# A 128-step recurrence: h's fold from three PSUM banks, its first triangles on ScalarE and GpSimd

## The chip, the cores and the metric

The program runs on one core of a Trainium2 chip. The metric is the time of one execution in device microseconds. "Before" is the median of three executions.

## What is computed

The reference is one block on x of shape (8, 128, 128): x plus causal latent attention over a recurrence of x, then plus six layers of window attention and gated feed-forward over a gated scan. Only the recurrence matters here:

```python
xw = einsum('ntd,dh->nth', x, Wx) + b
next_h = tanh(xw_t + prev_h @ Wh)      # 128 steps, 8 batches, D = 128
```

## The kernel before, in words

The kernel computes each step so that the sum over the 128 inputs is taken in a fixed order, one after another, with its roundings. For each output (a partition) and each of the 8 batches it needs the running sums of the products. It gets them in three parts: a **guess** (TensorE multiplies the weights by "triangles", copies of the step's vector masked so that column k holds the first k entries; one fp32 matmul gives all 128 prefix sums), a **rest** (the difference of neighbouring guesses is taken off the exact products, which TensorE makes from diagonal matrices of h or x, each split in an upper and a lower part), and the guess with its sign turned (**minus**). A reduction on VectorE, the **fold**, adds 3 x 128 numbers per batch, in the order rest, guess, minus. A program constant, OFFSET = 12, is added to guesses so that roundings fall where they should, and taken off again. Then VectorE evaluates tanh as a rational function with corrections.

There are two such sums per step: x's, which does not depend on h and is prepared a step ahead, and h's, which starts with x's result. Batches go in two halves of four. x's fold leaves its result where h's chain takes it in. PSUM has 8 banks of 512 columns: guesses of h in banks 0 and 1, rests of h in 2 and 3 (`REST_BANKS_H`), which x's guesses share (`SUM_BANKS_X`), x's rests in 4 and 6; small tiles of the tanh in 5 and 7. For the fold the three parts are laid side by side in SBUF (`adds`, in the space of the later layers' weights, stride 3).

Every engine has an order of its own, written by hand; semaphores join them. One step t:

- **VectorE**: `open_step` copies h to `h_now` (L1095), makes h's triangles of batches 0 and 1 (L1096), splits h in two parts (L1086, L1100). Then x's fold, first half (L1114), the difference of h's guesses, first half (L1108, L1109), x's fold, second half, four folds of h of two batches each (L1114, 128x768), tanh (L1130 to L1193). Its loop holds four steps; the others hold one.
- **ScalarE**: triangles of batches 2 and 3 (L783), h's guesses placed in `adds` (L798), `less_guess_of_h` (L803), lower diagonals of h, second half (L778), h's rests placed (`place_rests_h`, L821, 128x256 twice per half) with `place_minus_h` (L808) between; then for x of the next step, per half, the guess (L790) and its negative in the rest bank (L792), and last x's rests placed (L814).
- **TensorE**: h's guesses (`sums_h`, L1502), h's rests (`times`, L1487; the second half has first a matmul of the guess by the identity, L1551), x's guesses (`sums_x`, L1492, each after h's rest of that half has been placed), x's rests (L1512 and L1487), and `offset_h` (L1498), which opens the guess banks with the constant.
- **GpSimd**: h's triangles of the second half (L628), three diagonals of h (L642), h's copy to `hT` (L671), `minus_h` of the first half (L647), then for x, per half, triangles of step t + 2 (L628 again, after x's guess of that half), and per half the guess (L635) and its negative (L637) placed in `adds`.
- **SyncE** brings x's diagonals by DMA through a ring in HBM.

Behind the steps come latent attention and the layers, which the change does not touch, but for three reductions on VectorE at the end of the program (L1463 to L1467) whose result nobody uses.

## Time and profile before

| what | value |
|---|---|
| median of three runs | 3063.25 us (3061.85 to 3064.69) |
| the profiled execution's own time | 3067.32 us |
| its span | 3065.5 us |
| VectorE busy | 2690.4 us, 88% |
| PE (matmul) busy | 2581.4 us, 84% |
| GpSimd (POOL) busy | 2368.9 us, 77% |
| ScalarE (ACT) busy | 2261.6 us, 74% |
| mean granted TensorE clock | 0.986 |

The span runs from the first to the last instruction of the profiled execution. Busy times are of instructions in the engine; a matmul's row is longer than the time that it holds the queue, since the next one starts under it. The start of a row is in us from the span's start. "idle before <-releaser" is the time that the engine waited and whose result ended the wait.

### The profile page before, as it was taken

The page shows a single profiled execution, that of the slowest core. Times are in us where ns is not written, and L with a number is a line of the kernel's source. Part 1 is how long each engine was busy: PE and PEld are TensorE (multiplying, and loading weights), DVE is VectorE, ACT ScalarE, POOL GpSimd, SP SyncE. Part 2 cuts the span into 40 slices and gives each one's busy share as a digit, 9 for nine tenths or more (in the row PEclk, how much of TensorE's full clock was granted, in tenths as well). Part 3 has the DMA queues.
Part 4 walks back from the last instruction along what each step waited for, and adds up shares of the span by engine and source line. Part 5 has one row for each costly group of instructions (what it writes and reads, how often), then busy time and mean ns, then how long its engine had stood idle before and what let it go on. Part 6 is the DMA issues. An engine that isn't in the chain of part 4 may idle for free.

```text
span 3065.5 us, 51933 instructions
## 1 busy us (share of the span) xinstructions
PE 2581.4 (84%) x12402; PEld 1508.3 (49%) x12465; DVE 2690.4 (88%) x7345; ACT 2261.6 (74%) x4810; POOL 2368.9 (77%) x2545
## 2 busy tenths in 40 slices
PE   4878888887888888888878887876999999999997
PEld 2334433343433343333434333663666666667665
DVE  3999999999999999999999998656999999999996
ACT  3777777777777777777777776335888888888886
POOL 5777777777777777777777777007999999999994
PEclk9999999999999999999999999898999999999998
DMA  5333343333333333333333334200001010101000
GB/s 133 75 71 75 69 76 72 72 71 75 76 69 75 71 75 69 76 75 70 71 74 75 69 76 73 77 1 1 1 3 36 0 40 0 40 0 40 0 0 8
DMA packets 368014, 163.08 MB, mean 53 GB/s; under 512 B 285158, under 2 KB 298220, under 8 KB 367212
## 3 DMA queue, kind: packets, MB, share of 16 engines
q1 hardware_dynamic: 367980, 162.65, 25.7%
q8 instruction: 19, 0.31, 0.0%
q14 instruction: 15, 0.12, 0.0%
HBM read 156.81 MB, written 5.80 MB: 53 GB/s over the span
## 4 chain that ended last, share of the span: by engine, by line
DVE 33%; PE 22%; issue 20%; POOL 15%; ACT 6%; DMA 1%; POOLq 1%; SPq 1%; DVEq 0%; ACTq 0%
PE bank L1487 9%; POOL qk L714 8%; PE bank L1551 6%; DVE bank L1114 4%; PE bank L1502 4%; DVE bank L1109 3%; ACT qkv_w L798 3%; DVE sq L1089 3%; DVE bank L1089 3%; POOL rs L723 3%; DVE fix_trace L1180 3%; POOL qk L729 2%; ACT qkv_w L821 2%; DVE sq L1172 2%; DVE qkv_w L1114 1%
## 5 line engine op out<-in xcount | busy, mean ns | idle before, releaser
L628 POOL TENSOR_TENSOR kT<-upto,xT 128x512 f32<-128x512 f32 x260 | 270.1, 1039 | 380.8 <-PE bank L1492 380.8
L1114 DVE TENSOR_REDUCE bank<-qkv_w 128x2 f32<-128x768 f32 x512 | 466.1, 956 | 89.0 <-ACT qkv_w L821 74.1
L1487 PE MATMUL bank<-diag_h,w_part 128*128 128x512 f32 x1024 | 374.9, 488 | 161.5 <-DVE bank L1109 161.5
L1114 DVE TENSOR_REDUCE qkv_w<-qkv_w 128x4 f32<-128x1536 f32 x256 | 447.9, 1750 | 49.9 <-ACT qkv_w L814 32.7
L814 ACT COPY qkv_w<-bank 128x512 f32<-128x512 f32 x258 | 220.8, 856 | 255.3 <-PE bank L1487 255.3
L1487 PE MATMUL bank<-diag_x,w_part 128*128 128x512 f32 x1032 | 386.9, 496 | 13.4 <-DMA diag_x<-diag_ring 13.4
L642 POOL TENSOR_TENSOR diag_h<-eye,part 128x512 fp32r<-128x512 f32 x384 | 388.5, 1040 | 0.0
L1487 PEld LDWEIGHTS bank<-diag_h,w_part 128*128 128x128 f32 x1024 | 184.5, 190 | 410.4 <-issue 386.5
L1502 PE MATMUL bank<-qT,wh 128*128 128x256 f32 (+1 forms) x768 | 255.4, 468 | 149.8 <-DVE qT L1096 148.5
L723 POOL TENSOR_TENSOR rs<-rs,halfs 128x8 f32<-128x8 f32 x192 | 368.3, 1918 | 16.0
L1724 PE MATMUL bank<-qkv_w,xsT 128*128 (+1 forms) x576 | 308.6, 619 | 10.3 <-DVE rot_s L1336 8.0
L798 ACT ACTIVATE qkv_w<-bank,offset 128x512 f32<-128x512 f32 x256 | 230.8, 951 | 106.0 <-PE bank L1502 106.0
L1492 PE MATMUL bank<-kT,wx 128*128 128x512 f32 x516 | 276.6, 618 | 19.9 <-ACT qkv_w L821 19.9
L1512 PE MATMUL bank<-b,eye 128*128 128x512 f32 x516 | 273.9, 612 | 19.2 <-ACT bank L792 0.6
L635 POOL TENSOR_TENSOR qkv_w<-b,offset 128x512 f32<-128x512 f32 x258 | 269.2, 1043 | 14.6 <-ACT b L790 4.3
L1487 PEld LDWEIGHTS bank<-diag_x,w_part 128*128 128x128 f32 x1032 | 195.3, 189 | 161.7 <-issue 123.1
L821 ACT COPY qkv_w<-bank 128x256 f32<-128x256 f32 x512 | 214.5, 499 | 72.7 <-PE bank L1487 71.9
L714 POOL TENSOR_TENSOR qk<-rot_c,rot_s 128x512 f32<-128x512 f32 x192 | 244.2, 1272 | 25.9 <-DVE rot_s L1336 25.9
L1502 PEld LDWEIGHTS bank<-qT,wh 128*128 128x128 f32 x768 | 126.9, 188 | 235.4 <-DVE qT L1096 210.8
L637 POOL TENSOR_SCALAR qkv_w<-b 128x508 f32<-128x508 f32 x258 | 227.7, 882 | 17.5
L729 POOL TENSOR_TENSOR qk<-qk,rs 128x512 f32<-128x512 f32 x192 | 201.1, 1048 | 15.0
L790 ACT ACTIVATE b<-bank,offset 128x512 f32<-128x512 f32 x258 | 177.6, 688 | 25.5 <-PE bank L1492 19.0
(238 smaller groups left out, 6550.5 us busy)
## 6 DMA issues: line engine op xcount, KB each, us to landing
diag_x<-diag_ring SPq DMA_DIRECT2D x259, 512.0 KB, 7.2
qkv_w<-in_L_ffn_Wqkv SPq DMA_DIRECT2D x6, 1536.0 KB
diag_ring<-X SPq DMA_DIRECT2D x264, 4.0 KB, 5.6
diag_ring<-o_fin SPq DMA_DIRECT2D x8, 512.0 KB, 7.8
o_w<-in_L_ffn_Wo SPq DMA_DIRECT2D x6, 512.0 KB
w<-in_L_ffn_W SPq DMA_DIRECT2D x6, 341.0 KB
b<-in_L_ffn_b SPq DMA_DIRECT2D x6, 341.0 KB
w<-in_L_ffn_W SPq DMA_DIRECT2D x6, 128.0 KB
```

The lines of the kernel that those rows point to most:

```text
L628: pool.tensor_tensor(tri[n][:, rows, :], upto[:].unsqueeze(1).to_broadcast([P, 4, D]), src[:, rows].unsqueeze(2).to_broadcast([P, 4, D]), ...
L642: pool.tensor_tensor(diag[n][:, d, rows, :], eye[:].unsqueeze(1).to_broadcast([P, 4, D]), values.unsqueeze(2).to_broadcast([P, 4, D]), ALU ...
L714: pool.tensor_tensor(o, c_, s_[:, :, ::-1, :], ALU.add).then_inc(rot_sum, 1)
L723: link(pool.tensor_tensor(rs[:, c, :], rs[:, c, :], halfs[:, 0:8], ALU.pow), rs_ready, eight + (2 * c + 2))
L798: act.activation(adds[0][:, 4 * half:4 * half + 4, :, 1], bank[:, half, :].rearrange("p (n k) -> p n k", k=D), ACT.Identity, bias=offset[: ...
L821: act.copy(adds[0][:, rows, :, 0], bank[:, REST_BANKS_H[half], 2 * m * D:2 * m * D + 2 * D].rearrange("p (n i) -> p n i", i=D)).then_inc(r ...
L1114: return dve.tensor_reduce((pre, bias_at[0])[n][:, a:b], chain[n][:, a:b, :], AX_X, ALU.add)
L1487: return pe.matmul(dst, w_part[:, n, w], diag[n][:, d, a:b, :].rearrange("p n k -> p (n k)"), start=False, stop=True, skip_group_check=True)
L1492: pe.matmul(bank[:, SUM_BANKS_X[half], :], wx[:], tri[1][:, 4 * half:4 * half + 4, :].rearrange("p n k -> p (n k)"), start=True, stop=True ...
L1502: return pe.matmul(bank[:, half, (a - 4 * half) * D:(b - 4 * half) * D], wh[:], tri[0][:, a:b, :].rearrange("p n k -> p (n k)"), start=Fal ...
L1512: pe.matmul(rows, eye[:], guess_x[:, a:b, 0:D], start=False, stop=True, skip_group_check=True)
L1724: pe.matmul(bank[:, c % 2, :], xsT[:, par, :], w[:, at:at + BANK], start=True, stop=True).then_inc(qkv_ready, 1)
```

## The change

h's three parts stay in PSUM. Banks 0 and 3 hold its rests, 1 and 4 its guesses, 2 and 5 the negatives, and the fold of a half reads three neighbouring banks as one 128x4<-128x1536 reduction (`fold_h`). `place_rests_h`, GpSimd's `minus_h` and the four folds of two batches go; ScalarE writes both negatives to the PSUM banks (`place_minus_h`) and a contiguous copy of the guesses to SBUF (`copy_guess_h`). x's fold writes into the last column of the negatives' bank. The constant is taken off the guess by a one-row matmul (`less_offset_h`). x's rest banks are now 2 and 5, the small tiles' 6 and 7. `sums_x` waits for h's fold of the same half (`h_folded`). h's triangles of batches 0 and 1 are made by ScalarE in place of 2 and 3, those of 2 and 3 by GpSimd, ahead of its second half. VectorE's copy to `h_now` waits for `h_ready`. The three reductions at the end go. Renamed semaphores and x's index changes are left out below.

```diff
-REST_BANKS_H, REST_BANKS_X = (2, 3), (4, 6)
+REST_BANKS_H, GUESS_BANKS_H, MINUS_BANKS_H = (0, 3), (1, 4), (2, 5)
 SUM_BANKS_X = REST_BANKS_H
-OWN_BANKS = (5, 7)
+REST_BANKS_X = MINUS_BANKS_H
+OWN_BANKS = (6, 7)
...
-        adds = [qkv_w[:, n, :].rearrange("p (n i c) -> p n i c", n=NB, c=3) for n in range(2)]
-        bias_at = [tile[:, :, D - 1, 2] for tile in adds]
-        chain = [qkv_w[:, n, :].rearrange("p (n i) -> p n i", n=NB) for n in range(2)]
+        adds = qkv_w[:, 1, :].rearrange("p (n i c) -> p n i c", n=NB, c=3)
+        bias_at = adds[:, :, D - 1, 2]
+        chain = qkv_w[:, 1, :].rearrange("p (n i) -> p n i", n=NB)
+        guess_h = qkv_w[:, 0, 0:NB * D].rearrange("p (n k) -> p n k", n=NB)
...
+        minus_h = [bank_rows(which) for which in MINUS_BANKS_H]
+        links_h = [bank[:, first:first + 3, :].rearrange("p c (n k) -> p n k c", k=D) for first in REST_BANKS_H]
...
                 pool.wait_ge(h_static, this)
+                pool.tensor_tensor(tri[0][:, 2:4, :], upto[:].unsqueeze(1).to_broadcast([P, 2, D]),
+                                   h_now[:, 2:4].unsqueeze(2).to_broadcast([P, 2, D]), ALU.mult).then_inc(tri_h_mid, 1)
...
                 diagonal(0, 1, 0, part[:, 1, 0:4], diag_lower_h[0])
                 diagonal(0, 0, 1, part[:, 0, 4:8], diag_upper_h)
                 pool.tensor_copy(hT[:, :, bass.ds(value(pool, t + HT_AT), 1)].rearrange("p n a -> p (n a)"), h_now[:]).then_inc(h_ready, 1)
-                minus_h(counts[0])
                 later = at_step(value(pool, t + 2))
...
 
             def triangle_mid():
-                for n in (2, 3):
+                for n in (0, 1):
                     ins = act.activation(tri[0][:, n, :], upto[:], ACT.Copy, scale=h_now[:, n:n + 1])
-                ins.then_inc(tri_h_mid, 1)
+                ins.then_inc(tri_h_first, 1)
 
...
 
                 act.wait_ge(sum_ready[0], count)
-                act.activation(adds[0][:, 4 * half:4 * half + 4, :, 1], bank[:, half, :].rearrange("p (n k) -> p n k", k=D),
-                               ACT.Identity, bias=offset[:, 0:1], scale=1.0).then_inc(guess_placed, 1)
+                act.copy(guess_h[:, 4 * half:4 * half + 4, :], bank_rows(GUESS_BANKS_H[half])).then_inc(guess_copied, 1)
 
             def less_guess_of_h():
...
+                act.activation(bank[:, REST_BANKS_H[1], :], bank[:, GUESS_BANKS_H[1], :], ACT.Copy,
                                scale=-1.0).then_inc(less_guess_h, 1)
 
-            def place_minus_h():
-
-                act.activation(adds[0][:, 4:8, 0:D - 1, 2],
-                               bank[:, 1, :].rearrange("p (n k) -> p n k", k=D)[:, :, 0:D - 1], ACT.Identity,
-                               bias=offset[:, 1:2], scale=-1.0).then_inc(minus_placed[1], 1)
+            def place_minus_h(half):
+
+                act.activation(minus_h[half][:, :, 0:D - 1], bank_rows(GUESS_BANKS_H[half])[:, :, 0:D - 1], ACT.Copy,
+                               scale=-1.0).then_inc(minus_placed[half], 1)
 
...
+                copy_guess_h(0, counts[0])
+                act.wait_ge(split_h, this)
+                lower_h(4)
+                copy_guess_h(1, counts[1])
+                act.wait_ge(rest_placed_x, counts[1])
                 less_guess_of_h()
-                act.wait_ge(split_h, this)
-                lower_h()
-                place_rests_h(0, counts[0])
-                place_minus_h()
-                place_rests_h(1, counts[1])
-                act.wait_ge(sum_placed[1], counts[1])
-                act.wait_ge(rest_placed[1], counts[1])
+                act.wait_ge(diff_ready, this)
+                act.wait_ge(x_folded, this)
+                place_minus_h(0)
+                lower_h(6)
+                act.wait_ge(x_scanned, this)
+                place_minus_h(1)
+                act.wait_ge(sum_placed_x, counts[1])
+                act.wait_ge(rest_placed_x, counts[1])
                 take_sums_x(0, counts[2])
                 take_sums_x(1, counts[3])
...
+                    dve.wait_ge(h_ready, value(dve, this - 1))
                 dve.tensor_copy(h_now[:], h_own).then_inc(h_static, 1)
-                dve.tensor_tensor(tri[0][:, 0:2, :], upto[:].unsqueeze(1).to_broadcast([P, 2, D]),
-                                  h_own[:, 0:2].unsqueeze(2).to_broadcast([P, 2, D]), ALU.mult).then_inc(tri_h_first, 1)
                 n_u = upper(part[:, 0, :], h_own)
...
-                dst = bank[:, REST_BANKS_H[half], :].rearrange("p (n k) -> p n k", k=D)
-                placed = adds[0][:, 4 * half:4 * half + 4, :, 1]
-                dve.wait_ge(guess_placed, count)
-                dve.tensor_scalar(dst[:, :, 0:1], sums_[:, :, 0:1], -1.0, OFFSET, ALU.mult, ALU.add)
-                dve.scalar_tensor_tensor(out=dst[:, :, 1:], in0=sums_[:, :, 0:D - 1], scalar=-OFFSET, in1=placed[:, :, 1:],
-                                         op0=ALU.add, op1=ALU.subtract).then_inc(diff_ready, 1)
-
-            def fold(n, a, b):
-
-                return dve.tensor_reduce((pre, bias_at[0])[n][:, a:b], chain[n][:, a:b, :], AX_X, ALU.add)
+                rows = slice(4 * half, 4 * half + 4)
+                dst = bank_rows(REST_BANKS_H[half])
+                dve.wait_ge(guess_copied, count)
+                dve.tensor_scalar(dst[:, :, 0:1], guess_h[:, rows, 0:1], -1.0, None, ALU.mult)
+                dve.tensor_tensor(dst[:, :, 1:], bank_rows(GUESS_BANKS_H[half])[:, :, 0:D - 1], guess_h[:, rows, 1:],
+                                  ALU.subtract).then_inc(diff_ready, 1)
+
+            def fold_x(half):
+
+                rows = slice(4 * half, 4 * half + 4)
+                return dve.tensor_reduce(minus_h[half][:, :, D - 1], chain[:, rows, :], AX_X, ALU.add)
+
+            def fold_h(half):
+
+                return dve.tensor_reduce(pre[:, 4 * half:4 * half + 4], links_h[half], mybir.AxisListType.XY, ALU.add)
 
             def placed_x(halves):
-                dve.wait_ge(rest_placed[1], halves)
-                dve.wait_ge(sum_placed[1], halves)
+                dve.wait_ge(rest_placed_x, halves)
+                dve.wait_ge(sum_placed_x, halves)
 
             def products(dst, a, b):
...
-                    def placed_h(m):
-                        dve.wait_ge(rest_placed[0], quarters[m])
...
-                    fold(1, 4, 8).then_inc(x_scanned, 1)
-                    after(n_x)
-                    for m in range(4):
-                        placed_h(m)
-                        if m == 2:
-                            dve.wait_ge(x_scanned, this)
-                        n_h = step(fold(0, 2 * m, 2 * m + 2))
-                    after(n_h)
+                    fold_x(1).then_inc(x_scanned, 1)
+                    for half, done in ((0, x_folded), (1, x_scanned)):
+                        dve.wait_ge(done, this)
+                        dve.wait_ge(rest_ready[0], counts[half])
+                        dve.wait_ge(minus_placed[half], this)
+                        fold_h(half).then_inc(h_folded, 1)
+                    dve.wait_ge(h_folded, counts[1])
                     tanh()
                     open_step(value(dve, t + 2))
...
-            dve.tensor_reduce(small[:, 0:2], bank[0:SN, 0:3, 0:2 * D].rearrange("p c (n k) -> p n k c", k=D),
-                              mybir.AxisListType.XY, ALU.add)
-            dve.tensor_reduce(small[:, 2:4], bank[0:SN, 0:6:2, 0:2 * D].rearrange("p c (n k) -> p n k c", k=D),
-                              mybir.AxisListType.XY, ALU.add)
-            dve.tensor_reduce(small[:, 4:6], prob[0:SN, 0:6 * D].rearrange("p (c n k) -> p n k c", c=3, k=D),
-                              mybir.AxisListType.XY, ALU.add)
...
+            def less_offset_h(half):
+
+                return pe.matmul(bank[:, GUESS_BANKS_H[half], :], offset16[:, D:2 * D], offset16[:, 2 * D:], start=False,
+                                 stop=True, skip_group_check=True)
+
             def sums_h(half, a, b):
-                return pe.matmul(bank[:, half, (a - 4 * half) * D:(b - 4 * half) * D], wh[:],
+                return pe.matmul(bank[:, GUESS_BANKS_H[half], (a - 4 * half) * D:(b - 4 * half) * D], wh[:],
                                  tri[0][:, a:b, :].rearrange("p n k -> p (n k)"), start=False, stop=True,
                                  skip_group_check=True)
...
-                quarters = [value(pe, 4 * t + n) for n in (2, 4)]
                 pe.wait_ge(tri_h_first, this)
...
                 pe.wait_ge(tri_h_mid, this)
-                sums_h(0, 2, 4).then_inc(sum_ready[0], 1)
+                sums_h(0, 2, 4)
+                less_offset_h(0).then_inc(sum_ready[0], 1)
                 pe.wait_ge(tri_h_second, this)
-                sums_h(1, 4, 8).then_inc(sum_ready[0], 1)
+                sums_h(1, 4, 8)
+                less_offset_h(1).then_inc(sum_ready[0], 1)
 
                 for half in range(2):
...
                     else:
-                        pe.wait_ge(guess_placed, counts[1])
+                        pe.wait_ge(guess_copied, counts[1])
                         pe.wait_ge(less_guess_h, this)
-                        pe.matmul(bank[:, REST_BANKS_H[1], :].rearrange("p (n k) -> p n k", k=D)[:, :, 1:], eye[:],
-                                  adds[0][:, 4:8, 0:D - 1, 1], start=False, stop=True, skip_group_check=True)
-                    for d, made, count in ((0, diag_upper_h, counts[half]), (1, diag_lower_h[half], this)):
+                        pe.matmul(bank_rows(REST_BANKS_H[1])[:, :, 1:], eye[:], guess_h[:, 4:8, 0:D - 1], start=False,
+                                  stop=True, skip_group_check=True)
+                    for d, made, count in ((0, diag_upper_h, counts[half]), (1, diag_lower_h[half], (this, counts[1])[half])):
                         pe.wait_ge(made, count)
                         for w in range(2):
                             ins = times(bank[:, REST_BANKS_H[half], :], 0, w, d, 4 * half, 4 * half + 4)
                     ins.then_inc(rest_ready[0], 1)
                 for half in range(2):
-                    pe.wait_ge(rest_placed[0], quarters[half])
+                    pe.wait_ge(h_folded, counts[half])
                     sums_x(half, counts[2 + half])
                 for half in range(2):
                     rests_x(half, counts[2 + half], landed)
-                pe.wait_ge(minus_placed[1], this)
                 offset_h()
 
```

## Rows read from the trace of the kernel before

**Rows 1.** Busy time by engine (and instructions) in the steps' stretch, 39 to 1893.7 us.

```profile
39.00:1893.70 1854.70, 1495.21 (x4307) 732.56 (x4306) 1696.44 (x5694) 1360.82 (x2535) 1420.30 (x1520) 1.00 0.38 73
```

**Rows 2.** Line L1095: the whole run, then 500 to 1900 us.

```profile
L1095 DVE COPY h_now<-bank x129: 152/166/168, 13.0 to 1911.1; 128x8 f32<-128x8 f32 x129
...
L1095 DVE COPY h_now<-bank x97: 165/166/167, 501.7 to 1896.7; 128x8 f32<-128x8 f32 x97
```

**Rows 3.** Timeline of VectorE, one step: start us, us, what [idle before <-releaser].

```profile
1010.34 0.17 DVE L1095 COPY h_now<-bank 128x8 f32<-128x8 f32 x1
1010.42 0.41 DVE L1096 TENSOR_TENSOR qT<-upto,bank 128x256 f32<-128x256 f32 x1
...
1011.12 1.75 DVE L1114 TENSOR_REDUCE qkv_w<-qkv_w 128x4 f32<-128x1536 f32 x1
1013.05 0.17 DVE L1108 TENSOR_SCALAR bank<-bank 128x4 f32<-128x4 f32 x1 [0.17 <-ACT qkv_w L798]
...
1013.88 1.73 DVE L1114 TENSOR_REDUCE qkv_w<-qkv_w 128x4 f32<-128x1536 f32 x1
...
1018.14 1.82 DVE L1114 TENSOR_REDUCE bank<-qkv_w 128x2 f32<-128x768 f32 x2 [0.30 <-ACT qkv_w L821]
1020.00 0.17 DVE L1130 TENSOR_SCALAR bank<-bank 128x8 f32<-128x8 f32 x1
...
1024.84 0.17 DVE L1095 COPY h_now<-bank 128x8 f32<-128x8 f32 x1
```

**Rows 4.** Timeline of GpSimd (POOL), the same step.

```profile
1014.57 0.20 POOL L671 COPY hT<-h_now 128x8 f32 x1
1014.72 1.21 POOL L647 TENSOR_TENSOR qkv_w<-qkv_w,signs 128x508 f32<-128x508 f32 x1
...
1019.89 1.04 POOL L628 TENSOR_TENSOR kT<-upto,xT 128x512 f32<-128x512 f32 x1 [0.22 <-PE bank L1492]
...
1022.00 0.89 POOL L637 TENSOR_SCALAR qkv_w<-b 128x508 f32<-128x508 f32 x1
1022.97 1.04 POOL L635 TENSOR_TENSOR qkv_w<-b,offset 128x512 f32<-128x512 f32 x1
1024.08 0.87 POOL L637 TENSOR_SCALAR qkv_w<-b 128x508 f32<-128x508 f32 x1
```

**Rows 5.** Timeline of ScalarE (ACT), the same step.

```profile
1010.54 0.69 ACT L783 ACTIVATE qT<-upto,h_now 128x128 f32<-128x128 f32 x2 [0.48 <-DVE h_now L1095]
...
1013.71 0.65 ACT L803 ACTIVATE bank<-bank,offset 128x512 f32<-128x512 f32 x1
...
1017.61 0.85 ACT L821 COPY qkv_w<-bank 128x256 f32<-128x256 f32 x2 [0.56 <-PE bank L1487]
1018.47 0.69 ACT L790 ACTIVATE b<-bank,offset 128x512 f32<-128x512 f32 x1
...
1023.71 0.85 ACT L814 COPY qkv_w<-bank 128x512 f32<-128x512 f32 x1 [0.88 <-PE bank L1487]
```

**Rows 6.** Timeline of TensorE's matmuls (PE); first one matmul of L1492 alone.

```profile
1017.41 0.59 PE L1492 MATMUL bank<-kT,wx 128*128 128x512 f32 x1
...
1015.14 1.50 PE L1551 MATMUL bank<-qkv_w,eye 128*128 128x508 f32 x2
...
1018.59 1.12 PE L1492 MATMUL bank<-kT,wx 128*128 128x512 f32 x2 [0.15 <-ACT qkv_w L821]
...
1021.72 1.02 PE L1512 MATMUL bank<-b,eye 128*128 128x512 f32 x2
1022.17 1.50 PE L1487 MATMUL bank<-diag_x,w_part 128*128 128x512 f32 x4
1023.61 0.60 PE L1498 MATMUL bank<-offset 1*128 1x512 bf16 x2
```

**Rows 7.** Timeline at the program's end: reductions from PSUM, then from SBUF.

```profile
3059.10 0.94 DVE L1465 TENSOR_REDUCE small<-bank 64x2 f32<-64x768 f32 x1
3059.97 1.01 DVE L1467 TENSOR_REDUCE small<-prob 64x2 f32<-64x768 f32 x1
```

## What the change is expected to do

> **What bounds the kernel now.** I read the busy times of the recurrence's stretch first, then the period of its steps, then the timeline of one step engine by engine. In the stretch of the 128 recurrence steps VectorE is busy for 1696 of 1855 us, GpSimd for 1420, ScalarE for 1361 [rows 1]: VectorE leads, but nobody is free by much. The copy that opens a step (L1095) comes every (1896.7 - 501.7) / 96 = 14.53 us [rows 2]. The first two steps take what is left of 1898.1 us, 1898.1 - 126 x 14.53 = 67 us, and do something else (the ring is being filled); so 126 steps count.
>
> One step, from the copy at 1010.34 to that at 1024.84, is a nearly closed queue on VectorE [rows 3]: opening 0.78 (with 0.33 for the triangles of L1096), x's fold 1.75, difference 0.83 (from 1013.05 to 1013.88), x's other fold 1.73, four folds of h in two pairs of 1.82, then the tanh from 1020.00 to 1024.84, 4.84. Its waits are some 0.17 before the difference and such a 0.30 before each fold pair (the second pair is shown). A reader who stops here would say: VectorE bounds, take work from it.
>
> The other queue to read is GpSimd's [rows 4]. It handles x for step t+1 while VectorE does h of step t. Its triangle of x's second half waits for PE's sums (1018.59 + 1.12 = 1019.71 [rows 6]), and then four placements run to 1024.08 + 0.87 = 1024.95. The next step's h triangles are queued behind them, and the copy that releases these is at 1024.84. GpSimd is thus 0.1 us from being late.
>
> **The change, part by part.**
> VectorE loses the 0.33 of L1096 (two triangles); 2 x 1.82 + the 0.30 wait between the pairs become two folds of 128x4<-128x1536 from three banks. Their price: the same form at half length is there, 0.94 from PSUM and 1.01 from SBUF [rows 7]. A fold of 1536 takes 1.75 where one of 768 takes 0.955 (half of 1.82, plus the 0.045 of overlap), so 768 more elements cost 0.80, and I take 0.94 + 0.80 = 1.74 each, started 1.65 apart. Lower bound 1.65 (the SBUF fold less more than the PSUM gain of 0.07), upper 1.88 (twice 0.94). The Trainium skill (Perfetto Trace Analysis, Optimizing Scalar/DVE Operations) has an access overhead for VectorE of about 60 ns on SBUF and 125 on PSUM. By it, as an estimate, the two folds would cost 0.13 more per step, 16 us in all, and the time would be 3124; the two rows say the opposite for this very pattern, and I go by them.
> ScalarE loses the four strided placements of L821 that stood between PE and VectorE and the strided L798; its copies and negatives are now contiguous, 0.69 as L790 or 0.65 as L803 [rows 5]. Bounds 0.6 and 0.8 for the copies.
> PE reads the guess contiguously: two passes of L1551, with a stride of three, take 1.50, two of L1512 take 1.02 [rows 6], so some 0.46 is gained in its queue, where such a pass holds it for 0.43 (the 1.02 for two less the 0.59 of one, as at L1492). It adds two one-row matmuls (L1498: 0.60 for two, by estimate 0.23 in the queue and 0.37 to the end).
> GpSimd loses L647 (1.21), which stood in front of a wait anyway, worth nothing. It gains a triangle of 128x256 ahead of the one of 512: between 0.20 for 8 elements (L671) and 1.04 for 512 [rows 4], by length 0.61, in the queue 0.57; bounds 0.45 and 0.7. VectorE's new wait for h_ready is for a copy done 8 us earlier; only its own 0.05 or so counts, on an engine that will wait later in the step.
> **Moved:** PE's sums of x, half 1, waited for L821 (done 1017.61 + 0.85 = 1018.46) since it shares a bank with h's rest; now it waits for the second fold of h itself, the last thing before the tanh. Before, they were complete at 1019.71, 0.29 ahead of the tanh. Now they start 0.13 after the fold (as 1018.46 to 1018.59) and end 1.12 later, 1.25 after it. Behind them, in order, GpSimd's triangle and four placements, then the next step's h triangles, the later ones of which are on h's path. So x's loop closes through GpSimd:
>
> From the end of h's second fold,
> 1. to the end of x's sums: 0.13 + 1.12 = 1.25.
> 2. to GpSimd's next free start: 1024.95 - 1019.71 = 5.24, plus 0.08 (as from 1022.00 + 0.89 to 1022.97) = 5.32.
> 3. h's triangles, 0.57 + 1.04 = 1.61.
> 4. PE's second half: start 0.13 and first load 0.10 (as at L1492), two passes 0.86, one-row matmul 0.37 = 1.46.
> 5. ScalarE: start 0.04, guess copy 0.59 in the queue (0.69 less 0.10 of overlap), less_guess_of_h 0.57 (0.65 less 0.08), negative 0.65, 0.03 to VectorE = 1.88.
> 6. h's two folds, 1.65 + 1.74 = 3.39.
> Sum 14.91; I take 14.90. VectorE's own work in that period is 0.45 + 1.66 + 0.83 + 1.66 + 3.39 + 4.84 = 12.8, so it will wait about 2 us per step, nearly all of it before the difference. That wait also hides the 0.25 that VectorE's loop end costs in every fourth step (the mean of 14.53 against the 14.49 between the two copies of rows 3 has it), so 14.90 stands as the mean.
> Beside the steps: the three reductions at the end go (2.6 us, started 0.87 apart [rows 7]), and x's late last step adds about 1. Net -1.6.
> Change: (14.90 - 14.53) x 126 - 1.6 = 46.6 - 1.6 = +45. On the profiled execution, 3067.3 (span 3065.5 and 1.8 around it), that is 3112.3; the median of the runs stands 4.1 lower, so 3063.25 + 45 = 3108.
>
> **Rivals.**
> A, faster. GpSimd doesn't hold the loop (its spans are rough; its placements of x might really end earlier). Then x's loop closes through ScalarE: from h's last fold 0.13, PE's queue from L1492 to the last L1487 (1018.59 to 1023.67 is 5.08, less some 0.3 of waiting for ScalarE inside it: 4.8), then L814 0.04 + 0.75, the first triangles 0.69 (L783), PE 0.06 + 0.96 + 0.37 (its restart, four passes of 256 columns, the one-row matmul), copy 0.04 + 0.69, difference 0.11 + 0.66, x's fold 1.66, h's folds 3.39: 14.35 by rounding. That is -0.18 x 126 - 1.6 = -24, so 3039. It decides once GpSimd is 0.5 us faster. For it: VectorE's 2 us of slack. Against: the 0.1 us between GpSimd's last placement and the next step. 0.12.
> B, slower still. The eye matmul on the guess keeps the price of L1551, 0.66 a pass, since its output skips columns. Then h's second rest comes last: from the end of less_guess_of_h 0.05 + (0.86 + 0.46) + 1.10 (L1487's 1.50 less the 0.40 that its first lies under the pass before it) + 0.09 = 2.56 to the second fold, where the forecast has 0.58 + 0.03 + 1.65 = 2.26. So 0.30 more: 15.20, 0.67 x 126 - 1.6 = +83, 3146. 0.12.
> C, the folds at 1.88 instead of 1.74: 0.28 more, 15.18, 0.65 x 126 - 1.6 = +80, 3143. 0.08. Folds of 1.55 would be needed for no change; with the lower bounds of folds, triangle and copies together (-0.18, -0.12, -0.09) the period is 14.51 and the time 3063 - 4 = 3059. That all-low end, 0.06, is my "no change".
> The change does do what it says: L1096 and L821 are off VectorE's path in it; only the removed wait comes back elsewhere.
>
> **How the numbers follow.** Forecast 0.62, A 0.12, B 0.12, C 0.08, all-low 0.06. Most likely 3108. A measurement of this kernel tells 0.2%, 6 us, from no change. Faster by more: A, with 0.01 of the all-low end, 0.13. Same: 0.05. Slower: 0.82. The range leaves out A and the lower half of the all-low end below (0.15) and what lies above the centres of B and C (some 0.05): from 3062, which takes in the forecast with one or two lower bounds (folds at 1.65 and the triangle at 0.45: 14.60, 3070), to 3150.
>
> **What would show it.** In the profile after, per step: the copy to h_now every 14.9 us; VectorE idle 1.5 to 2 us before the difference, released by ScalarE's guess copy; GpSimd's first h triangle starting some 1.4 us after h_now's copy, not 0.25, with no idle time before it; PE's sums of x half 1 waiting for VectorE's fold for about 0.9 us; folds of 1.74; the busy time of VectorE down. Wrong, if GpSimd idles before h's triangles (A), if the rest of h's second half releases the last fold (B), if folds differ from 1.74 (C).

## The result and the profile after

The changed kernel takes 3273.4 us (median of 4 runs, 3271.4 to 3279.3) against 3063.4: 1.0687 times as long, 95% interval 1.0674 to 1.0700. That is 210 us more, where 45 were forecast. All ratios leave out executions in the chip's slower state or over 1.5% above the fastest of their kernel (two of the ten with the triangles back, 3121 and 3417 us, and one of the thirteen of the kernel before beside them, 4359). The head of its page, with the granted clock of TensorE in 40 slices:

```profile
span 3269.2 us, 51129 instructions
...
PE 2856.2 (87%) x12721; PEld 1586.1 (49%) x12721; DVE 2611.4 (80%) x6957; ACT 1980.4 (61%) x4426; POOL 2294.4 (70%) x2546
...
PEclk9889898899889988998899889998899999999999
```

VectorE, ScalarE and GpSimd are busy for less time than before, TensorE for 275 us more, and its granted clock, 1.00 in the steps before [rows 1], is 0.89 in them now. The stretches by themselves (columns as in [rows 1]: length, busy time of PE, PEld, DVE, ACT, POOL, then PEclk, DMA share, GB/s): the steps (but for the first 3 us of the 126), 6.8 us and 8.0 us of one step, and a whole other step.

```profile
80.30:2119.90 2039.60, 1754.61 (x4531) 805.88 (x4531) 1610.91 (x5289) 1074.43 (x2140) 1339.22 (x1510) 0.89 0.32 65
907.97:914.79 6.82, 6.82 (x13) 2.86 (x11) 3.42 (x4) 3.82 (x9) 3.77 (x5) 0.50 0.32 77
914.79:922.81 8.02, 6.89 (x22) 3.61 (x21) 7.28 (x35) 3.37 (x6) 4.33 (x5) 1.00 0.02 6
937.67:952.54 14.87, 12.65 (x37) 5.64 (x37) 12.76 (x43) 8.56 (x18) 10.65 (x13) 1.00 0.35 71
```

The copy to `h_now` (L1097 now, count, duration, first and last start) between 500 and 1700 us:

```profile
L1097 DVE COPY h_now<-bank x73: 165/166/168, 516.1 to 1683.5; 128x8 f32<-128x8 f32 x73
```

So a step takes 16.21 us on average, against 14.53 [rows 2]. No step does. Of the 126 intervals between copies behind the first two, 62 are 14.8 to 14.9 us, 62 are 17.5 to 17.7 and two are between; and there are 64 stretches at the clock's lower level, 1.2 GHz, 430 us in all, one for each interval that isn't one of the short ones. The account: 126 x (14.86 - 14.53) = 42 us from the steps that are not disturbed, 126 x (16.21 - 14.86) = 170 us from the clock; the first two steps end 3 us earlier, and what lies behind the steps is 5 us shorter (the three reductions, 2.7, in it). Sum 204, the difference of the spans.

**The undisturbed step** is the one that was forecast. VectorE from one copy to the next, with the two folds of h in the row at 944.23, then the tanh:

```profile
937.67 0.17 DVE L1097 COPY h_now<-bank 128x8 f32<-128x8 f32 x1
...
941.73 0.17 DVE L1107 TENSOR_SCALAR bank<-qkv_w 128x4 f32<-128x4 f32 x1 [1.85 <-ACT qkv_w L805]
...
942.39 1.75 DVE L1114 TENSOR_REDUCE bank<-qkv_w 128x4 f32<-128x1536 f32 x1
944.23 3.43 DVE L1118 TENSOR_REDUCE bank<-bank 128x4 f32<-128x1536 f32 x2
947.69 0.17 DVE L1134 TENSOR_SCALAR bank<-bank 128x8 f32<-128x8 f32 x1
...
952.53 0.17 DVE L1097 COPY h_now<-bank 128x8 f32<-128x8 f32 x1
```

GpSimd: h's triangles (256 columns, then 512), x's triangle of the second half, x's last placement; then ScalarE: the second guess copy and the first negative:

```profile
938.42 0.89 POOL L648 TENSOR_SCALAR qkv_w<-b 128x508 f32<-128x508 f32 x1
939.39 0.61 POOL L672 TENSOR_TENSOR qT<-upto,h_now 128x256 f32<-128x256 f32 x1
939.96 1.04 POOL L639 TENSOR_TENSOR qT<-upto,h_now 128x512 f32<-128x512 f32 x1
...
949.09 1.04 POOL L639 TENSOR_TENSOR kT<-upto,xT 128x512 f32<-128x512 f32 x1 [0.61 <-PE bank L1483]
...
953.28 0.88 POOL L648 TENSOR_SCALAR qkv_w<-b 128x508 f32<-128x508 f32 x1
```

```profile
942.53 0.59 ACT L805 COPY qkv_w<-bank 128x512 f32<-128x512 f32 x1 [0.25 <-PE bank L1494]
...
943.53 0.56 ACT L814 ACTIVATE bank<-bank 128x508 f32<-128x508 f32 x1
```

TensorE in the same step, from offset_h to x's second sums:

```profile
937.57 0.60 PE L1489 MATMUL bank<-offset 1*128 1x512 bf16 x2
939.11 0.70 PE L1498 MATMUL bank<-qT,wh 128*128 128x256 f32 x2 [0.94 <-ACT qT L790]
940.05 0.70 PE L1498 MATMUL bank<-qT,wh 128*128 128x256 f32 x2 [0.25 <-POOL qT L672]
940.68 0.38 PE L1494 MATMUL bank<-offset 1*128 1x512 bf16 x1
941.05 1.12 PE L1498 MATMUL bank<-qT,wh 128*128 128x512 f32 x2
942.11 0.38 PE L1494 MATMUL bank<-offset 1*128 1x512 bf16 x1
...
947.79 1.12 PE L1483 MATMUL bank<-kT,wx 128*128 128x512 f32 x2 [0.55 <-DVE bank L1118]
```

VectorE waits 1.85 us for ScalarE's guess copy [rows 3 had 0.17 there]. GpSimd starts on h's triangles 1.72 us after the copy (939.39 against 937.67) because its placement of x only ends at 939.31. PE's second sums of x wait 0.55 for the fold. VectorE has no idle time from the difference at 941.73 to the end of the folds: x's second fold ends at 944.14, ScalarE's negative at 944.09.

**The long step.** The same instructions of TensorE, 32 us earlier, where the clock fell to 1.2 GHz at 907.97, 2.7 us after the copy at 905.24:

```profile
907.66 0.96 PE L1498 MATMUL bank<-qT,wh 128*128 128x256 f32 x2 [0.28 <-POOL qT L672]
...
909.09 2.08 PE L1498 MATMUL bank<-qT,wh 128*128 128x512 f32 x2
...
911.63 2.07 PE L1478 MATMUL bank<-diag_h,w_part 128*128 128x512 f32 x4
913.50 1.66 PE L1548 MATMUL bank<-qkv_w,eye 128*128 128x508 f32 x2
```

The pair of 512 columns takes 2.08 in place of 1.12, h's four rest matmuls 2.07 in place of some 1.2, the pair on the guess 1.66 in place of 1.09. All of it is on h's path, and the step is 17.57 us long.

### The profile page after: what moved, and what is told of

It reads as the page before. It is cut to its first block, busy times and chain, and to the rows that moved or that the text cites. A ratio compares the mean times of both kernels' runs of the same rounds, so it can differ in the third digit from the quotient of the medians.

```text
span 3269.2 us, 51129 instructions
## 1 busy us (share of the span) xinstructions
PE 2856.2 (87%) x12721; PEld 1586.1 (49%) x12721; DVE 2611.4 (80%) x6957; ACT 1980.4 (61%) x4426; POOL 2294.4 (70%) x2546
## 4 chain that ended last, share of the span: by engine, by line
POOL 32%; PE 30%; issue 17%; DVE 16%; ACT 2%; POOLq 2%; DMA 1%; SPq 1%; DVEq 0%; ACTq 0%
DVE bank L1118 10%; POOL qkv_w L646 8%; PE bank L1498 7%; POOL qkv_w L648 7%; POOL qk L721 6%; PE bank L1478 6%; PE bank L1483 4%; DVE bank L1114 3%; PE bank L1548 3%; PE bank L1494 3%; POOL qT L672 2%; POOL kT L639 2%; POOL rs L730 2%; POOL qk L736 2%; ACT qkv_w L805 1%
## 5 line engine op out<-in xcount | busy, mean ns | idle before, releaser
L639 POOL TENSOR_TENSOR kT<-upto,xT 128x512 f32<-128x512 f32 x260 | 270.6, 1041 | 682.6 <-PE bank L1483 682.5
L1118 DVE TENSOR_REDUCE bank<-bank 128x4 f32<-128x1536 f32 x256 | 445.5, 1764 | 157.4 <-PE bank L1478 151.5
L1498 PE MATMUL bank<-qT,wh 128*128 128x256 f32 (+1 forms) x768 | 391.3, 596 | 153.6 <-ACT qT L790 119.2
L1114 DVE TENSOR_REDUCE bank<-qkv_w 128x4 f32<-128x1536 f32 x256 | 449.5, 1756 | 49.4 <-ACT qkv_w L819 48.6
L1478 PE MATMUL bank<-diag_h,w_part 128*128 128x512 f32 x1024 | 424.4, 544 | 8.0 <-DVE bank L1108 0.2
L1483 PE MATMUL bank<-kT,wx 128*128 128x512 f32 x516 | 283.7, 632 | 128.7 <-DVE bank L1118 128.7
L805 ACT COPY qkv_w<-bank 128x512 f32<-128x512 f32 x256 | 150.3, 587 | 385.0 <-PE bank L1494 385.0
L819 ACT COPY qkv_w<-bank 128x512 f32<-128x512 f32 x258 | 221.9, 860 | 201.7 <-PE bank L1478 201.7
L1478 PEld LDWEIGHTS bank<-diag_h,w_part 128*128 128x128 f32 x1024 | 225.9, 236 | 177.3 <-issue 123.6
L646 POOL TENSOR_TENSOR qkv_w<-b,offset 128x512 f32<-128x512 f32 x258 | 269.5, 1045 | 14.8 <-ACT b L797 4.4
L1508 PE MATMUL bank<-b,eye 128*128 128x512 f32 x516 | 264.0, 593 | 0.6 <-ACT bank L799 0.6
L1483 PEld LDWEIGHTS bank<-kT,wx 128*128 128x128 f32 x516 | 82.1, 189 | 270.4 <-issue 265.4
L1107 DVE TENSOR_SCALAR bank<-qkv_w 128x4 f32<-128x4 f32 x128 | 21.5, 168 | 239.5 <-ACT qkv_w L805 239.5
```

Source lines behind the costliest of these rows:

```text
L639: pool.tensor_tensor(tri[n][:, rows, :], upto[:].unsqueeze(1).to_broadcast([P, 4, D]), src[:, rows].unsqueeze(2).to_broadcast([P, 4, D]), ...
L646: pool.tensor_tensor(adds[:, rows, :, 1], src, offset[:, 0:1].unsqueeze(2).to_broadcast([P, 4, D]), ALU.add)
L1114: return dve.tensor_reduce(minus_h[half][:, :, D - 1], chain[:, rows, :], AX_X, ALU.add)
L1118: return dve.tensor_reduce(pre[:, 4 * half:4 * half + 4], links_h[half], mybir.AxisListType.XY, ALU.add)
L1478: return pe.matmul(dst, w_part[:, n, w], diag[n][:, d, a:b, :].rearrange("p n k -> p (n k)"), start=False, stop=True, skip_group_check=True)
L1483: pe.matmul(bank[:, SUM_BANKS_X[half], :], wx[:], tri[1][:, 4 * half:4 * half + 4, :].rearrange("p n k -> p (n k)"), start=True, stop=True ...
```

## The experiments

All have the changed kernel as their base, but for two that say so. "Full" matmuls are of 128 rows and 512 bf16 columns; none of them computes anything that is used. The operands of these are made by GpSimd at the start, so each kernel with them also waits for that once, ahead of the loop (`pool_up`); the diffs leave it out.

**The clock, 1.** Edit, in TensorE's loop:

```diff
+            def filler(which, times_):
+                for _ in range(times_):
+                    pe.matmul(bank[:, which, :], eye16[:], masks[:, 0, :], start=True, stop=True, skip_group_check=True)
...
                 offset_h()
+                filler(SUM_BANKS_X[0], 4)
```

> The changed kernel with four bf16 matmuls of 128 rows and 512 columns (eye16 by masks, into the bank of x's first guess, which nobody reads then) behind offset_h, in the 0.94 us in which TensorE otherwise waits for h's first triangles. They take some 0.9 us there and compute nothing that is used. Theory 1 (the steps of 17.5 us are those in which TensorE's granted clock is at its lower level, and it falls because of what TensorE does, or doesn't do, around that gap): the clock is 1.00 through the steps, nearly all of them take 14.86 us, and the time is 3105 to 3115. Theory 2 (the long steps have another cause, a DMA or a queue, and the low clock only goes with them): 3270 as before the edit.

Measured: 3104.3 us, 1.013 times before (1.0113 to 1.0147). All 126 steps take 14.8 or 14.9 us, and the clock never falls in them:

```profile
80.30:1951.10 1870.80, 1708.28 (x5036) 750.20 (x5036) 1605.07 (x5289) 1074.14 (x2140) 1340.02 (x1512) 1.00 0.36 71
```

0.9 us of work that nobody uses, in every step, makes the program 169 us faster. Theory 2 is out. What is left is near the forecast: 38.5 us more than the kernel before beside it (3065.8), where 45 were forecast.

**The clock, 2: what kind of work.** Edit: in `filler`, the operands of offset_h, `offset16[:, 0:D], offset16[:, 2 * D:]`.

> The changed kernel with four one-row matmuls (the form of offset_h: one row of weights, 512 bf16 columns) in the gap in place of the four with 128 rows. They hold TensorE's queue for as long, with one row of the array's 128 at work. If what keeps the clock up is that TensorE isn't waiting: 3104 and a clock of 1.00, as with the full ones. If it is work in the array's rows: the clock falls as in the changed kernel, 3200 to 3280. I expect the second with 0.6.

Measured: 3277.2 (ratio 1.0704, 1.0686 to 1.0722), 64 low stretches, 434 us of them:

```profile
80.30:2121.00 2040.70, 1862.80 (x5029) 851.93 (x5028) 1610.70 (x5278) 1074.40 (x2138) 1338.94 (x1509) 0.89 0.33 65
```

TensorE's rows in the profile are 108 us busier than in the changed kernel, and the clock is as low. Filling the gap with this kind of work does nothing for it; with matmuls of 128 rows the clock stays up (run before).

**The clock, 3: how much.** Edit: `filler(SUM_BANKS_X[0], 1)`.

> The changed kernel with one full matmul in the gap in place of four: how much work it takes. If 0.2 us of work in every step are enough, all steps are 14.86 and the time is 3104; if they are not, the share of long steps is between that of the changed kernel (half of them) and none: 3105 to 3250.

Measured: 3160.2 (1.0315, 1.0298 to 1.0333); 32 low stretches (164 us) instead of 64, in an execution of 3170. One matmul takes the clock's cost from 169 us to 56.

**The clock, 4: where.** Edit:

```diff
                     sums_x(half, counts[2 + half])
+                    if half == 0:
+                        filler(GUESS_BANKS_H[0], 3)
```

> The changed kernel with three full matmuls between x's first sums and its second, where TensorE waits 0.55 us for h's last fold (into a guess bank that is read out by then), and none ahead of the triangles. If the amount of full-row work in a step keeps the clock up: near 3104, few or no long steps. If its place does (it must lie next to the gap ahead of the triangles, behind which the clock falls): as the changed kernel, 3250 to 3280. They end 0.1 us before the second sums could start, so they cost nothing themselves.

Measured: 3273.5 (1.0671, 1.0653 to 1.0689), 64 low stretches, 430 us:

```profile
80.30:2121.00 2040.70, 1823.47 (x4783) 843.12 (x4908) 1612.06 (x5281) 1074.73 (x2141) 1339.00 (x1511) 0.89 0.34 65
```

Three full matmuls between x's sums change nothing; one in the gap ahead of h's triangles takes off two thirds of the loss. So the place matters, and not only the sum per step.

**The clock, 5: where it is up anyway.** Base: the kernel before, four full matmuls behind its offset_h.

> The kernel before with the four matmuls behind offset_h. Its clock is at 1.00 through the steps, so they can gain nothing: 3063, or up to 3080 if they delay h's first guess, which starts 1.2 us after offset_h there.

Measured: 3065.3 (0.9997, 0.9987 to 1.0006). Where the clock is up, the four matmuls neither gain nor cost anything.

**The triangles back.** Edit: L672 and its semaphore off GpSimd, ScalarE's loop at batches 2 and 3 again, L1096 of the kernel before back on VectorE.

> The changed kernel with the triangles as they were: VectorE makes those of batches 0 and 1, ScalarE those of 2 and 3, GpSimd only its second half. Theory 1 (x's loop through GpSimd sets the period; the 0.57 us of the added GpSimd triangle lie on it): undisturbed steps of 14.25 us in place of 14.86, and h's first guess starts 0.55 after the copy to h_now instead of 1.44, so that TensorE's gap there is shorter and the clock falls less often or never: 3025 if never, up to 3190 if as often as now. Theory 3 (VectorE bounds): the period grows by the 0.33 of its triangles.

Measured: 3101.9 us as the median of all ten executions; the eight that the ratio takes (1.0088, 1.0057 to 1.0118) lie between 3066 and 3106, with a mean granted clock from 0.971 to 0.956. So how often the clock falls differs here from one execution to the next. In the profiled one (3101): 89 steps of 14.3, 37 longer ones (15.4 to 17.1), 37 low stretches with 184 us. VectorE does more and each undisturbed step is 0.57 shorter: GpSimd's 0.57.

TensorE's start of a step in which the clock fell (at 1012.86):

```profile
1009.93 0.60 PE L1489 MATMUL bank<-offset 1*128 1x512 bf16 x2
1010.58 0.70 PE L1498 MATMUL bank<-qT,wh 128*128 128x256 f32 x2
1011.47 0.70 PE L1498 MATMUL bank<-qT,wh 128*128 128x256 f32 x2 [0.19 <-ACT qT L788]
...
1012.85 2.07 PE L1498 MATMUL bank<-qT,wh 128*128 128x512 f32 x2 [0.36 <-POOL qT L639]
```

The wait of 0.94 is gone, the longest one here is 0.36, and the clock falls all the same. So that wait can't be the whole cause.

**Both.** Edit: this one and `filler(SUM_BANKS_X[0], 4)`.

> Both edits: triangles as they were, and the four bf16 matmuls behind offset_h. Here they can delay h's first guess by some 0.3 us, as it could start 0.55 after the copy. Theory 1: clock at 1.00 through the steps, 14.25 to 14.5 us each, 3025 to 3055, faster than the kernel before. Theory 2: no different from the second of these kernels.

Measured: 3033.3 us (0.9896, 0.9880 to 0.9913), 126 steps of 14.29, none disturbed. The change without its triangles, with the clock up, is 1% faster than the kernel before.

**The triangles alone.** Base: the kernel before, with the triangles as in the change, its own fold.

> The kernel before with only the triangles moved (ScalarE 0 and 1, GpSimd 2 and 3 ahead of its half), the fold as it was. Theory 1: 14.9 us per step, because h's guesses come 0.4 to 0.55 us later and four copies still stand between TensorE and VectorE, while the 0.33 saved on VectorE is not on the path: about 3110 if the clock stays up, more if it falls. Theory 3 (VectorE bounds): 14.2 us per step, 3020.

Measured: 3167.3 us (1.0341, 1.0324 to 1.0358): 64 steps of 14.8 or 14.9, 62 longer, 62 low stretches (253 us). With 0.33 us per step taken off VectorE, the undisturbed step is 0.34 longer, and the clock adds 0.48 more on average. GpSimd isn't the reason here: it starts on h's triangles 0.25 us after the copy in every step, as in the kernel before. TensorE's first guess starts 0.94 us after the copy (1000.42 against 999.48), released by ScalarE's triangles, where it started 0.55 after it (1010.89 against 1010.34) on VectorE's; the chain of the profile runs from there over ScalarE's guess, the difference, h's rests and the folds to the tanh. So this half of the change costs time by itself, in both ways.

**The moved wait, first try.** To free x's sums from h's folds, x's guesses need banks that are not h's. Edit of the control: `own` takes its tiles from SBUF.

> Control for the next one: the changed kernel with the four matmuls in the gap (3104 us, all steps 14.86) and the tanh's small tiles in SBUF instead of PSUM banks 6 and 7. The tanh's operations keep their lengths within 0.02 us each, and VectorE has about 2 us of waiting in a step: 14.86 per step and 3104 by the theory that x's loop sets the period. If these tiles cost VectorE more, still no change up to 2 us per step, as its wait takes it up.

Measured: 3809 us (1.2442, 1.2421 to 1.2463). The tanh of a step, then GpSimd at the same time:

```profile
1017.42 1.08 DVE L1090 TENSOR_TENSOR f_part<-own_sb,f_part 128x72 f32<-128x72 f32 x1
1018.42 1.01 DVE L1087 TENSOR_SCALAR den_upper<-own_sb 128x8 int32<-128x8 int32 x1
1019.35 0.16 DVE L1087 TENSOR_SCALAR own_sb<-own_sb 128x8 int32<-128x8 int32 x1
```

```profile
1017.29 1.12 POOL L640 TENSOR_TENSOR kT<-upto,xT 128x512 f32<-128x512 f32 x1 [1.19 <-PE bank L1484]
1018.38 1.04 POOL L647 TENSOR_TENSOR qkv_w<-b,offset 128x512 f32<-128x512 f32 x1
```

Operations of 72 and 8 elements, 0.22 and 0.15 us in the kernel before, take a full microsecond. They end at 1018.50 and 1019.43, right behind the ends of GpSimd's instructions (1018.41 and 1019.42). The tanh takes 8.3 us instead of 4.8 in nearly every step. The Trainium skill (SBUF — State Buffer, Who interferes with whom) says that a VectorE instruction with two SBUF inputs contends with a GpSimd instruction that reads SBUF, through the shared read interface. The first row fits that; the second reads one SBUF tile only and is held as well. The expectation was wrong.

The longer tanh isn't all of the 705 us. The step is 20.48 us on average, 5.62 more than with the tiles in PSUM, and 3.5 of these are the tanh's. For the rest there is the clock, which is low once in each of the 126 steps, for 1041 us in all:

```profile
80.94:2661.50 2580.56, 2056.28 (x5040) 980.58 (x5040) 2116.49 (x5293) 1097.24 (x2142) 1357.68 (x1512) 0.80 0.26 52
```

The four full matmuls are there, but TensorE now waits 2.9 to 3.8 us behind them for h's triangles. How the 705 us divide between the two wasn't measured.

> As the control, with banks 6 and 7 now given to x's guesses, so that sums_x doesn't wait for h's folds; ScalarE's write of the negative into x's rest bank waits for the fold instead. This takes away the one wait to which the forecast put its 1.5 us of lateness. Theory 1 (the wait of x's second sums for h's last fold sets the period through GpSimd): 13.61 us per step, 1.25 less, so 3104 - 158 = 2947. Theory 3 (the added reductions or VectorE set it): 14.86 and 3104 as in the control.

> x's guesses in banks of their own, the triangles as in the kernel before, and two of the full matmuls in the gap. Theory 1: VectorE is now the bound, with waits of 0.1 us left; 13.21 us per step, 2896 in all (14.29 and 3033 without the first edit). If the clock falls with two matmuls only: some steps of 15 us or more and 2930 to 3000.

Measured: 3811 and 3814 us (1.2442 and 1.2452). Their steps take 20.48 and 20.49 us, with one low stretch in each, as in the control; the long tanh and the clock hide what these two were to tell. (In them x's sums, which open a PSUM bank for adding, no longer go through h's rest banks and nothing else opens those, so part of h's rest is left out; the later ones open bank 3 ahead of the loop.)

**The moved wait, second try.** Edit, on top of the four full matmuls:

```diff
-SUM_BANKS_X = REST_BANKS_H
+SUM_BANKS_X = (REST_BANKS_H[0], 7)
-OWN_BANKS = (6, 7)
+OWN_BANKS = (6, REST_BANKS_H[1])
...
                 for half in range(2):
-                    pe.wait_ge(h_folded, counts[half])
+                    if half == 0:
+                        pe.wait_ge(h_folded, counts[0])
                     sums_x(half, counts[2 + half])
```

with `fix_keep` and `q_keep` in bank 6, `f_guess` and `z_part` in bank 3, and a wait for the fold ahead of ScalarE's negative of x and of offset_h.

> The changed kernel with the four matmuls in the gap (3104, steps of 14.86), where x's second guess gets PSUM bank 7, so that its sums no longer wait for h's last fold; ScalarE's negative in x's rest bank waits for the fold instead. All small tiles of the tanh stay in PSUM: most in bank 6, f_guess, z_part and den_part in bank 3, which is free during the tanh. The arithmetic is the same. This undoes the one step to which the blind working put the lateness. Theory 1: GpSimd is no longer held up, the period is 14.06, and the time 3104 - 0.80 x 126 = 3003. Theory 3 (folds or VectorE set the period): 14.86 and 3104.

Measured: 3029.6 us (0.9893, 0.9877 to 0.9910), 14.27 per step. The wait is worth 0.59 us per step, 75 us, not the 0.80 expected: with GpSimd freed, another loop ends last. The chain of the profile over one step (start, us, what):

```profile
1005.17 0.97 PE bank L1496 x4
1006.14 1.09 PE bank L1504 x4
1007.23 0.33 PE bank L1500
...
1007.59 0.59 ACT qkv_w L807
...
1012.55 1.14 PE bank L1485 x2
...
1014.30 0.66 ACT bank L801
...
1015.09 1.10 PE bank L1514 x2
```

From h's first fold it runs over x's sums, ScalarE's negative of x, TensorE's queue with x's rests and the four added matmuls (L1496) to h's first guess, its copy, the difference and the folds. That is nearly the loop of rival A (14.35); GpSimd isn't in it. ScalarE's triangles end at 1006.05, so that without the added matmuls little would be gained.

**The two together.**

> As the one before, with the triangles made as in the kernel before, and three matmuls in the gap. Theory 1: 13.64 us per step against 14.29 with the triangles back alone, so 3033 - 0.65 x 126 = 2951, clock at 1.00.

> As the second of these, without any matmul in the gap. By the undisturbed steps 13.6 us and 2950. TensorE's work is packed in a shorter step, so the clock should fall less than with the triangles back alone (a mean of 0.95 in its steps), but h's first guess still waits for the triangles: 2950 to 3030.

Measured: 2972.9 (0.9707, 0.9691 to 0.9723) and 2972.6 us (0.9703, 0.9687 to 0.9719), 13.84 per step in both. Both are 0.20 us per step longer than the 13.64 expected, and the chain runs over TensorE and ScalarE again. Without any added matmul, where a fall to 0.95 in the steps was expected, the clock stays up, here in all steps and then between 500 and 1700 us the copies:

```profile
80.30:1820.00 1739.70, 1573.81 (x4526) 725.46 (x4527) 1644.48 (x5406) 1062.34 (x2139) 1261.85 (x1383) 1.00 0.38 76
...
L1097 DVE COPY h_now<-bank x87: 165/166/167, 506.7 to 1696.6; 128x8 f32<-128x8 f32 x87
```

This version, the change's fold, the old triangles, x's second guess in a bank of its own, is 3.0% faster than the kernel before and 9% faster than the changed one.

## Why the prediction was wrong

The time, 3273, is outside 3062 to 3150. The direction was right.

- **What bounded the kernel before**: right in that VectorE's queue was not the whole story. Taking 0.33 off it made the kernel slower (the triangles alone), but by a path that the working didn't price: ScalarE's triangles let h's first guess start 0.39 later, while GpSimd was on time; the profile's chain in the kernel before runs along h in the same way. That GpSimd had 0.1 us to spare is read rightly (its last placement ends at 1024.95, 0.11 behind the copy); that run doesn't test it. (The two copies of [rows 3] are 14.50 apart, not 14.49; nothing hangs on it.)
- **The moved wait**: right, and the cause of the undisturbed steps. By the forecast's items, in the step at 937.67: from the fold's end (944.23 + 3.43) to the end of x's sums 1.25 (forecast 1.25); to GpSimd's next start 5.33 (5.32); triangles 1.61 (1.61); TensorE's second half 941.00 to 942.49, 1.49 (1.46); ScalarE and hand-overs, to the fold at 944.23, 1.74 (1.88, its guess copy took 0.59 and its negative 0.56, contiguous to contiguous); folds 3.43 (3.39). Sum 14.85 (14.91), measured 14.86. ScalarE was 0.14 quicker than forecast and no longer last: VectorE, busy from the difference on, is free for the fold at 944.14, the negative is there at 944.09. So the profile's chain leaves GpSimd after its first triangle and runs over h's first guess, the difference and x's fold; in time the two paths are 0.05 apart, and that the forecast's one gives the period is in part luck. VectorE's wait before the difference is 1.85 (about 2), GpSimd's first triangle starts 1.72 after the copy (some 1.4), the wait of x's second sums is 0.55 (about 0.9). With the wait gone the step is 0.59 shorter.
- **The folds**: 1.766 us each for 1.74; the half-length rows [rows 7] had the price, and rival C is out. Rival B is out too: the pair on the guess takes 1.09 with its load, not 1.50. Rival A is out: GpSimd doesn't idle before h's triangles, in any step. Once it is freed, something near A's loop does set the period (the second try).
- **Beside the steps**: -1.6 forecast, -8 in these two profiled executions (the first two steps -3, behind the steps -5). Some of it is spread: with the four matmuls the kernel before has 1150.7 us behind its steps, where its own profile has 1154.4.
- **The step that failed** is a term that the working put at nothing without saying so: each duration of TensorE was taken from rows at 1.00 of the clock [rows 1] and carried over, as if the level were a property of the kernel. All three rivals, and the range, were about waits and prices at full clock. The level fell to 1.2 GHz 64 times, and the clock's share of the loss is 170 of the 212 us in the steps; four full matmuls in the gap gave 169 back.

Where to look for it: TensorE's rows around the start of a step before and after. Before, h's first guess and what follows it (six passes):

```profile
1010.89 1.99 PE L1502 MATMUL bank<-qT,wh 128*128 128x256 f32 x6 [1.17 <-DVE qT L1096]
1014.10 1.20 PE L1487 MATMUL bank<-diag_h,w_part 128*128 128x512 f32 x4 [1.22 <-DVE bank L1109]
```

Both kernels wait about 1 us behind offset_h (before, from 1009.72 to 1010.89; after, from 938.17 to 939.11), and before there are another 1.2 us of waiting ahead of 1014.10, and the clock stays up. So it isn't the longest gap. Nor is it the sum: TensorE's rows fill 81% of the steps' stretch before [rows 1] and 85% of the undisturbed step after. But before, six passes stand together, 1.7 us of full-row work; after, the triangles come one by one from ScalarE and GpSimd, and from 937.57 to 941.05 TensorE does four passes of 256 columns, 0.86 us, and three one-row matmuls, between waits of 0.94 and 0.25. That this spreading is what lets the clock fall is not shown. Against it as the whole reason: with the triangles back the first guesses stand close together again (0.19 and 0.36 between them) and the clock still fell in 37 steps; with them alone, the six passes stand together (1000.42, no wait inside) behind a wait of 1.60, and it fell in 62. The forecast itself had this schedule: the first guess late by 1, the halves a GpSimd triangle apart. It was read only for what waits on TensorE, not for what TensorE does.

The Trainium skill (TensorE: Matmul & The Clock Gate, HAM oscillation) tells of the same loop of a starved engine that starts cold again and again, there with gaps of microseconds from DMA waits. The run with the small tiles in SBUF agrees: waits of 2.9 to 3.8 us, and the clock falls in each step. In the changed kernel the clock falls again and again too, but the long idle gaps of which that section warns aren't there: its longest wait of TensorE is 0.94 in an undisturbed step and 1.13 in a long one; a reader who goes by them would have passed it.

What stays open: why the clock falls in this schedule, and how much full-row work, and how close to which gap, is enough. The runs give points (none, one and four matmuls; three in another place), not a rule. And in which of the steps the clock falls was not tried.

## What to carry to other kernels

When a change delays or spreads what TensorE does, even on an engine that isn't the bound, write down its full-row work through the step, and give "the clock falls" a rival with its own price: here 2.7 us per disturbed step. The cheap test is a few unused full matmuls in the gap: if the time drops and the granted clock rises, it was the clock. If nothing changes, the gap may be the wrong one, as between x's sums, or the matmuls too few for it, as with the tiles in SBUF. And before work is taken off the busiest engine, look for the engine whose queue closes right at the step's start: GpSimd's added 0.57 us lengthened the step by 0.57, more than the 0.33 taken from VectorE could bring.

## What the runs showed of the hardware that was not expected

- TensorE's clock fell to 1.2 GHz with no wait of the engine over 0.94 us between the step's start and the fall (1.13 in any step), its rows busy for some 85% of the undisturbed step (12.65 of 14.87), while the kernel before kept 2.4 GHz with 81% and waits of up to 1.5 us; with the triangles back it fell with none over 0.40 between the step's start and the fall. In the gap of 0.94, four one-row matmuls didn't help (3277), one full one took off two thirds of the loss (3160), four all of it (3104), three in another gap did nothing (3273).
- Some VectorE operations of 8 to 72 elements took 1.0 us instead of 0.15 to 0.22 when all their operands were in SBUF and GpSimd was at work; the tanh took 8.3 us instead of 4.8. The program took 3809 us against 3104, the low clock of that run included.
- ScalarE's contiguous copy from PSUM to SBUF took 0.59 where the one with a bias took 0.69, and one with a bias and an output stride of three (L798 before) 0.95.
